# A two-layer kernel's tile loop: the expert number of each tile read once, a tile ahead

## The reference

```python
attn = softmax(q[..., :, None] * k[..., None, :], axis=-1)
logits = einsum('bsej,bsj->bse', attn, v).reshape(-1, E)
top_logits, idx = top_k(logits, 2)
scores = softmax(top_logits)
for e in range(8):
    h1 = x_rep @ w1[e].T                 # 128 -> 2 * 352
    a, g = split(h1, 2)
    out += where(expert_ids == e, silu(a) * g @ w2[e].T, 0)
combined = (out * scores).reshape(N, 2, 128).sum(axis=1)
```

## Time and profile before

| | |
|---|---|
| median of 3 runs | 447.51 us (446.91 to 449.23) |
| profiled execution, first to last instruction | 447.6 us |
| the same execution's own time | 449.39 us |
| mean granted TensorE clock | 0.892 of full speed |
| VectorE busy | 351.8 us, 79% |
| TensorE matmul busy | 339.3 us, 76% |
| ScalarE busy | 262.3 us, 59% |
| GpSimd busy | 243.6 us, 54% |

### The profile page before, as it was taken

One profiled execution on the slowest core, in us unless ns is written; L12 is line 12 of the kernel. 1 busy time (PEld: TensorE's weight loads), 2 busy tenths in 40 slices (PEclk: granted clock), 3 DMA queues, 4 the chain that ended last, 5 costly groups with the idle time before them and its releaser, 6 DMA issues. The chain is left out here.

```text
span 447.6 us, 5679 instructions
## 1 busy us (share of the span) xinstructions
PE 339.3 (76%) x1491; PEld 242.7 (54%) x1491; DVE 351.8 (79%) x611; ACT 262.3 (59%) x443; POOL 243.6 (54%) x247
## 2 busy tenths in 40 slices
PE   1846669947797698998800986979798898989785
PEld 0436449637786587888700552535555554545453
DVE  5779999887897496957419777788999988988945
ACT  2478673554647556565431589767478578678320
POOL 4464500531576377678840000058888888889840
PEclk9986985856899699998965899898899999999989
DMA  6365200110111011311041001005677867755873
GB/s 174 98 189 145 53 0 2 30 30 7 36 48 42 24 43 51 86 42 32 31 149 58 0 0 36 13 6 99 115 142 156 164 125 142 146 111 107 171 141 94
DMA packets 36212, 35.09 MB, mean 78 GB/s; under 512 B 12165, under 2 KB 30838, under 8 KB 36182
## 3 DMA queue, kind: packets, MB, share of 16 engines
q0 software_dynamic: 7104, 21.90, 23.7%
q1 hardware_dynamic: 29078, 12.84, 10.7%
HBM read 13.29 MB, written 4.65 MB: 40 GB/s over the span
## 5 line engine op out<-in xcount | busy, mean ns | idle before, releaser
L1257 DVE TENSOR_TENSOR_SCAN state<-dec,win_t 128x1024 f32<-128x1024 f32 x32 | 83.6, 2634 | 2.4 <-ACT dec L836 1.4
L845 ACT ACTIVATE sil<-psum,vec_t 128x512 f32<-128x512 f32 x64 | 43.1, 687 | 47.5 <-PE psum L308 47.4
L610 POOL TENSOR_SCALAR state<-state,ssm_cb 128x1024 f32<-128x1024 f32 x32 | 63.7, 1991 | 3.6 <-POOL sel_now L587 2.5
L557 POOL DMA_INDIRECT parts<-t_out,part x39 | 41.6, 1067 | 40.4 <-ACT t_out L780 31.2
L1569 PE MATMUL psum<-hid,g_w 128*128 128x512 f32 x128 | 60.0, 596 | 0.0
L1268 DVE TENSOR_TENSOR hid<-sil,psum 128x512 f32<-128x512 f32 x64 | 41.7, 678 | 17.7 <-ACT sil L845 10.1
L1561 PE MATMUL psum<-cw_hl,sel_now 128*128 128x512 f32 x64 | 38.0, 594 | 15.5 <-DVE hid L1268 12.7
L545 POOL DMA_INDIRECT x_tile<-normed,token x39 | 41.7, 1069 | 13.3 <-issue 10.0
L1154 DVE TENSOR_TENSOR t_hid<-t_sil,psum 128x352 f32<-128x352 f32 x39 | 20.3, 521 | 27.8 <-ACT t_sil L764 24.5
L771 ACT ACTIVATE t_hid_t<-psum 128x384 f32<-128x384 f32 x39 | 19.2, 491 | 37.7 <-PE psum L1424 37.7
L1435 PE MATMUL psum<-w_out,t_hid_t 128*128 x234 | 37.4, 299 | 1.5 <-ACT t_out L780 1.1
(11 more groups left out here) (301 smaller groups left out, 860.8 us busy)
## 6 DMA issues: line engine op xcount, KB each, us to landing
xn_tok<-state POOLq DMA_DIRECT2D x32, 512.0 KB, 4.7
e_raw<-in_L_ffn_w SPq DMA_DIRECT2D x16, 128.0 KB, 2.2
both<-parts SPq DMA_DIRECT2D x4, 512.0 KB, 5.3
e_raw<-in_L_ffn_w SPq DMA_DIRECT2D x8, 176.0 KB, 2.4
res<-in_L_attn_x SPq DMA_DIRECT2D x4, 256.0 KB, 3.7
normed<-rows SPq DMA_DIRECT2D x1, 1024.0 KB, 5.5
g_raw<-in_L_ffn_w SPq DMA_DIRECT2D x16, 64.0 KB, 2.1
g_w<-in_L_ffn_w SPq DMA_DIRECT2D x16, 64.0 KB, 2.3
```

What stands on the lines that cost most here:

```text
L557: pool.indirect_dma_start(out=parts, out_offset=bass.IndirectOffsetOnAxis(ap=part[:, n:n + 1], axis=0), in_=t_out[n % ORING][:, :], in_off ...
L610: own(pool.tensor_scalar(state[k % 4][:, :], state[k % 4][:, :], ssm_cb[:, k // 2:k // 2 + 1], 0.0, ALU.mult, ALU.add))
L845: act.activation(sil[c % SRING][:, :], ps[c % 2][:, :], ACT.Silu, bias=vec_t[:, V_B1 + c // NBLK:V_B1 + c // NBLK + 1]).then_inc(h_silu, 1)
L1257: dve.tensor_tensor_scan(state[k % 4][:, :], dec[(k // 2) % DECS][:, at_half], win_t[:, at_half], 0.0, ALU.mult, ALU.add).then_inc(scanned, 1)
```

## The change

The expert number is no longer read at the head of `hidden(n)` and again at the head of `output(n)`. Tile 0's is read once ahead of the loop, behind the last of the waits there. In turn n, behind `hidden(n)` and ahead of `turn_hidden(n - 2)`, the number of tile n + 1 is read; it stays in a register until `output(n + 1)` has used it, three turns after `hidden(n + 1)`. The number of reads falls from 78 to 39. Matmuls, transposes, waits between engines and the other engines' instructions stay as they are.

```diff
@@ -1386,8 +1386,11 @@
-            def expert_of(n):
-                return bass.ds(pe.value_load(tile_e[0:1, n:n + 1], min_val=0, max_val=E0 - 1), 1)
+            expert = {}
+
+            def load_expert_of(n):
+
+                expert[n] = bass.ds(pe.value_load(tile_e[0:1, n:n + 1], min_val=0, max_val=E0 - 1), 1)
 
@@ -1398,7 +1401,7 @@
             def hidden(n):
 
-                e = expert_of(n)
+                e = expert[n]
                 pe.wait_ge(x_lo_ready, n + 1)
@@ -1427,7 +1430,7 @@
             def output(n):
 
-                e = expert_of(n)
+                e = expert.pop(n)
                 pe.wait_ge(h_copied, n + 1)
@@ -1455,11 +1458,14 @@
             pe.wait_ge(pads_ready, 1)
+            load_expert_of(0)
             for n in range(-2, NTILE + 3):
                 if n + 2 < NTILE:
                     turn_x(n + 2)
                 if 0 <= n < NTILE:
                     hidden(n)
+                if 0 < n + 1 < NTILE:
+                    load_expert_of(n + 1)
                 if 0 <= n - 2 < NTILE:
                     turn_hidden(n - 2)
                 if n >= 3:
```

## The result

| | before | after |
|---|---|---|
| median (measured side by side, 4 runs each) | 447.21 us (446.77 to 449.23) | 441.3 us (440.58 to 442.48) |
| profiled execution, first to last instruction | 447.6 us | 440.7 us |
| VectorE busy | 351.8 us, 79% | 351.2 us, 80% |
| TensorE matmul busy | 339.3 us, 76% | 338.3 us, 77% |
| GpSimd busy | 243.6 us, 54% | 241.7 us, 55% |

The ratio is 0.986 (95% interval 0.982 to 0.989): 5.9 us faster, where 442.5 us was forecast. Medians in this document are over all runs of a kernel, ratios over its fast ones alone: one of the ten runs of the first experiment, two of the first four with the early first read and three of the twelve of the relieved kernel before lay over 1.5% above that kernel's fastest, and without them those medians are 446.77, 438.5 and 444.2 us. Busy times hardly moved. What moved is idle time inside the loop.

What follows compares the result with a forecast made beforehand. GpSimd ends the loop, and TensorE's queue, with two exposed reads a turn, releases its sends late. Send 13's lead of 2.86 us plus 2.17 us of vanished wait gave 5.0 us: 442.5 us by the median, range 439.8 to 446.3.

Steps and rivals of the forecast that it cites:

- The reads and their price: TensorE's queue: 39 reads, 0.65 us each and covered behind hidden; tile 0's read delays the first turn_x by 0.86 us.
- Turns 2 to 12: Loop's early turns: lead -0.21 us at turn 2, 0.44 at turn 5, held at 0.44 by busy VectorE through turn 12.
- `turn_x(14)` to sine work: ScalarE's sine work would start 2.67 us behind turn_x(14), where it was 3.27, and lead by 1.46 us.
- Send 13 and the wait that falls away: GpSimd: send 13 leads by 2.86 us, and 2.17 us of the wait ahead of send 21 falls away.
- Sine work of turn 22: ScalarE: turn_x(24) follows VectorE's split at 164.7, sine work comes 2.67 us later at 167.4, a lead of 4.6 us.
- TensorE's result 21: Stalled turn 24 adds 0.65 us to the sine work's lead of 4.6: a lead of 5.25 us for send 21.
- GpSimd's own time behind send 13: GpSimd's sends and fetches to the last send: no change in the sum, transfers counted as 1 us of the range.
- Hidden anyway: Rival: TensorE's reads already hide behind queued work, or the number is made again at each use: 447.5 us, chance 0.05.
- VectorE takes it back: Rival: lead made only in turns 2, 5, 14 and 16, less the first read: 1.7 us, 445.8 us, chance 0.19.
- Larger gain: Rival: turn 16's low-clock stretch shrinks or send 13 stops limiting, send 12 limits: 7.2 us, 440.3 us, chance 0.15.
- Slower by the clock: Rival: TensorE's granted clock falls to half after short waits, 1.45 us lost per such turn: 450 to 454 us, chance 0.08.

Runs made afterwards that it cites:

- the first experiment: Kernel before with the expert number read once per tile, at the head of hidden in the tile's own turn, kept until output: 446.81 us (10 runs), 0.997 of before.
- the early first read: Changed kernel with tile 0's read moved right behind the wait for the tile table: 442.34 us (4 runs) and 442.88 us (6 runs).
- the relieved kernel before: Kernel before, its 78 reads kept, with GpSimd's filling of sel moved to where GpSimd waits: 445.17 us (12 runs), 0.995 of before.
- the second pair: Second profiled executions of the kernel before and the changed kernel, both unchanged: 447.82 us (one run) and 441.46 us (6 runs).
- The experiment with the reciprocals: Changed kernel with eight of VectorE's sixteen scans replaced by one-input reciprocals of the same length in time, the mixer's linear scan left out: 445.02 us (one run).
- the two reads a tile ahead: Changed kernel's place with 78 reads, the number read twice per tile behind hidden, a tile ahead: 447.56 us (10 runs), 0.999 of before.
- the first variant with the early selects: Changed kernel with GpSimd's memset and both selects for sel done ahead of its first send: 439.91 us (4 runs), 0.980 of before.

## Why the prediction was right, and where it was off

**The reads and their price: right.** 39 reads; the first at 0.497 us; first `turn_x` later by 0.88 us on the loop's clock (-0.86). The distance of 0.1 us between the queue's `turn_x` and `hidden` held where TensorE doesn't stall. Behind a stall it is 0.25 us, and the transposes wait up to 0.3 us more, 4.3 us in 22 times. So the cover for the moved read is not quite whole, but GpSimd's pace hides that.

**Turns 2 to 12: right in the path, slightly low in one term.** (The turn of the earlier trace rows, called 26, is turn 27; nothing hangs on its number.) -0.24 against -0.21 and 0.49 against 0.44; then 0.77 from turn 6 on where I let VectorE hold the lead at 0.44. In the second pair the lead at turn 5 is -0.07 and at turn 6 0.14. The difference of 0.3 us is thus within what two executions of one kernel differ by. `turn_x(14)` to sine work is 2.92 us for 2.67, the 0.25 us of the stalled turn that I had not counted; the sum came to 1.52 against 1.46.

**Send 13 and the wait that falls away: right.** 2.88 against 2.86, and send 21 is unstalled. That step I had as the likeliest limit, and it was.

**Sine work of turn 22: 4.2 for 4.6, and TensorE's result 21: 6.15 for 5.25.** The first is smaller because `turn_x(24)` did not wait for VectorE's split, as the prediction had it: the split ended 0.6 us before it, TensorE came to it without idle from its own work, with a lead of 3.6 us for 4.1. The second is the larger because before had a stretch at half clock just there which after lacks (us; busy us of each engine; granted clock):

```profile
176.90:180.40 3.50, 3.50 (x17) 3.43 (x16) 3.08 (x6) 1.11 (x5) 1.05 (x2) 0.51 0.42 110
```

The second execution of before lacks it too, and against that one the result leads after's first by only 4.2 us. Nothing depended on it, since GpSimd was later in after.

**The mis-sized term: GpSimd's own time behind send 13.** I carried 2.86 + 2.17 = 5.0 us to the last send as if GpSimd's work kept its length. Measured in the first pair: 2.88 + 2.17 + 1.91 = 6.96. From send 21 to send 38 it took 46.25 us before (47.08 in the second execution) and 44.5 in all three of after, 1.7 us less in the first pair; the other 0.2 us lie between sends 13 and 21. GpSimd's transfers in that stretch (number; busy us, mean ns; idle), before and after:

```profile
L557 POOL DMA_INDIRECT parts<-t_out,part x18 | 19.5, 1084 | 8.1 <-issue 4.0 <-ACT t_out L780 2.5 <-POOL sw_lo L526 0.8
L545 POOL DMA_INDIRECT x_tile<-normed,token x8 | 9.3, 1157 | 2.6 <-issue 1.5 <-PE psum L1397 0.6 <-POOL ssm_cb L567 0.5
```

```profile
L557 POOL DMA_INDIRECT parts<-t_out,part x18 | 18.6, 1034 | 5.9 <-issue 3.7 <-POOL sw_lo L526 0.8 <-ACT t_out L780 0.6
L545 POOL DMA_INDIRECT x_tile<-normed,token x8 | 8.8, 1094 | 2.6 <-issue 1.8 <-POOL ssm_cb L567 0.5 <-PE psum L1400 0.3
```

The mean transfer is 50 to 63 ns shorter, with the count the same: the 25 of them from send 21 to just ahead of send 38 took 27.80 us and take 26.39, which is 1.4 us; 0.3 us is GpSimd's other work. Three of them differ by 1.4 together, and the small differences of the others cancel: those that began inside lines 1117, 1130 and 1132 took 1.37, 1.91 and 1.72 us and take 1.00, 1.08 and 1.54. The prediction had named transfers "of 0.97 and some of 1.6 us" as 1 us of its range and put nothing into the sum. The experiment with the reciprocals shows that a scan is what stretches one of them. That they meet the scans later in after, because the two engines now stand otherwise to each other, is read from the traces of five executions and not set by hand; it is an accident of this schedule and no rule.

Part of the near hit is luck. The 2.17 us are those of one execution of before, in which a half-clock stretch lay just ahead of send 21; in the second that send waited 1.27 us, which makes the term 0.97, and its last send leads by 3.41 + 0.97 + 2.70 = 7.08 us. So the term was high by up to 1.2 us while GpSimd's own time, put at nothing, gave 1.9 to 2.7, and the median fell by 5.9 where the loop gained 6.8.

**Leads against the medians.** The loop gained 6.8 us; the medians 5.9 us. In the first pair of traces the spans differ by 6.9 us: 6.96, less 0.97 of a later start of the loop, plus 0.9 behind the last send. Those two terms are no part of the loop and vary between executions, as the second pair shows: 7.1 us of lead at the last send and 4.8 of span.

**The rivals.** *Hidden anyway* fell with the result, and why is shown by the two reads a tile ahead: a lead of queued work can't be built when the queue itself needs 2.7 us a turn. That was the Trainium skill's rule (Advanced Engine Details and Errata, Sequencer Loop and Engine Queue Depths); it holds here only where other work precedes the read, as in the earlier trace rows and behind `hidden` in after. *VectorE takes it back*: it does hold the lead flat from turn 6 to turn 11 (0.77 us throughout), but turns 12 to 14 go through TensorE's chain again. *Larger gain* by a vanished half-clock stretch: the one around the stall of turn 16 stayed, and send 13 stayed the limit. *Slower by the clock*: it didn't come. The granted clock of after, by stretch (us; busy us of each engine; clock), against the earlier trace rows:

```profile
109.60:147.10 37.50, 31.37 (x208) 26.66 (x206) 30.86 (x49) 26.77 (x62) 25.43 (x24) 1.00 0.15 44
147.10:153.90 6.80, 4.76 (x19) 4.65 (x20) 5.09 (x8) 3.46 (x10) 2.16 (x2) 0.50 0.08 20
153.90:218.80 64.90, 57.35 (x397) 50.68 (x395) 48.44 (x87) 39.89 (x103) 51.92 (x48) 1.00 0.17 49
```

It is at 2.4 GHz but for the stall of 4 us ahead of turn 16 and what follows it, as before. Waits of 1 to 2 us at `turn_x` did not lower it here. In the first execution of before, 3.4 us at half clock followed three such waits (1.86, 1.29 and 1.22 us, at turns 5, 24 and 33), in the second none; what decides it no run shows.

## What to carry to other kernels

When an engine idles with "issue" as the reason and its next instruction waits for no semaphore, count what its queue runs between two dispatches: here register reads of 0.65 us each made a turn of 2.65 us out of 2.1 us of work. Fewer of them helps only together with a place in which queued work covers those that stay, and ahead of a loop the first one belongs where the engine still has something to do. Follow the gain to the engine that ends the stage and look at once at what that engine does late in it and could do earlier: here moving a memset of 1.8 us and two selects of 2.4 on GpSimd, with the early first read, took the median from 441.46 to 436.89 us, 3.4 us of it in the loop.

## What the runs showed of the hardware

An indirect DMA issued by GpSimd that starts inside a VectorE instruction with two operands in SBUF lasts some 0.8 us plus what is left of that instruction: 1.91 us with 1.09 us of a scan left (208.57 against 209.66), 1.60 with 0.80 left (161.34), 1.47 with 0.62 of a product left (169.09 in before). Beside a reciprocal, with one operand, it lasts 0.97 (the very first fetch, ahead of the loop, 1.21 to 1.23 in every trace). One that begins 0.04 us behind the start of a scan is not held: it took 0.97 us (128.17 in before), and the scan 1.30 where others take 1.22. The Trainium skill (SBUF — State Buffer, SBUF: two separate sides) says that the ports which VectorE shares with GpSimd are an exclusive lock: whichever starts first, a VectorE instruction with two SBUF inputs or a GpSimd one that reads SBUF, has them for its whole length. The runs agree, with an indirect DMA as the GpSimd instruction; that it reads SBUF then is not shown by itself. The same section's warning on DMAs issued from GpSimd speaks only of VectorE's faster two-port modes.

The reverse shows in the first variant with the early selects: VectorE's 0.69 us became 2.71 beside a select that reads SBUF, and a one-input TENSOR_SCALAR went from 0.42 to 1.76 us. And the first read of a register from SBUF on TensorE costs 0.5 us and each later one 0.3, with 0.15 us of register work behind it, in every trace of this study (0.493 to 0.498 us for the first, 0.300 to 0.304 for the median).
